# The masked keys' term of a causal attention, made from turned values, a reversed scan and a spread weight

## What is computed

```python
att = jnp.einsum('bhqd,bhkd->bhqk', q, k) / np.sqrt(HEAD_DIM)
causal = jnp.tril(jnp.ones((T, T), dtype=bool))
att = jnp.where(causal, att, 0.0)
att = jax.nn.softmax(att, axis=-1)
out = jnp.einsum('bhqk,bhkd->bhqd', att, v)
```

## Time and profile before

| | us |
|---|---|
| median of 3 runs (1337.8 to 1341.09) | 1340.07 |
| span of the profiled execution, first to last instruction | 1332.9 |
| median less that span | 7.2 |
| token stage, up to the attention's first matmul | 268.6 |
| PE busy | 1165.0 (87%) |
| DVE busy | 949.8 (71%) |
| ACT busy | 747.9 (56%) |
| POOL busy | 364.2 (27%) |
| mean granted TensorE clock | 0.950 |

### The profile page before, as it was taken

One profiled execution on the slowest core, in us unless ns is written; L12 is line 12 of the kernel. 1 busy time (PEld: TensorE's weight loads), 2 busy tenths in 40 slices (PEclk: granted clock), 3 DMA queues, 4 the chain that ended last, 5 costly groups with the idle time before them and its releaser, 6 DMA issues.

```text
span 1332.9 us, 26802 instructions
## 1 busy us (share of the span) xinstructions
PE 1165.0 (87%) x7680; PEld 508.3 (38%) x7680; DVE 949.8 (71%) x1921; ACT 747.9 (56%) x1553; POOL 364.2 (27%) x716
## 2 busy tenths in 40 slices
PE   2999488889998799879896999699879996999998
PEld 1666355433343243324332333233323332333345
DVE  5777388878688668866785689568766885689822
ACT  1544233256765576557564766476547664766673
POOL 6121011333323132413132223222232233224221
PEclk9999699989999899989997999799889998999999
DMA  2446933371007100810063006300540054002023
GB/s 87 142 158 169 178 111 111 111 92 45 6 1 98 43 6 3 97 43 6 4 82 59 6 2 79 62 6 3 65 77 6 2 64 77 6 2 73 5 84 115
DMA packets 59124, 79.55 MB, mean 60 GB/s; under 512 B 6112, under 2 KB 48480, under 8 KB 57952
## 3 DMA queue, kind: packets, MB, share of 16 engines
q1 hardware_dynamic: 57824, 73.56, 27.8%
q0 software_dynamic: 1152, 4.19, 1.0%
HBM read 43.78 MB, written 29.36 MB: 55 GB/s over the span
## 4 chain that ended last, share of the span: by engine, by line
PE 56%; DMA 10%; DVE 7%; issue 3%; ACT 2%; SPq 1%; DVEq 1%; ACTq 0%; POOL 0%; POOLq 0%
PE ps_s L1046 16%; PE ps_o L1060 16%; PE ps_m L209 14%; DMA q_op<-shift_t 10%; DVE part_max L220 5%; PE ps_o L1070 2%; PE ps_m L1092 2%; PE ps_m L213 2%; ACT probs L928 2%; PE ps_x L1037 1%; PE ps_x L1038 1%; DVE row_max L233 1%; DVE turned L963 1%; SPq L775 1%; PE ps_x L1023 1%
## 5 line engine op out<-in xcount | busy, mean ns | idle before, releaser
L220 DVE TENSOR_REDUCE part_max<-ps_m 128x1 f32<-128x512 f32 (+3 forms) x1200 | 669.1, 603 | 249.0 <-PE ps_m L213 130.7
L928 ACT ACTIVATE probs<-ps_s 128x512 f32<-128x512 f32 (+3 forms) x1280 | 614.0, 535 | 365.2 <-PE ps_s L1046 359.9
L1046 PE MATMUL ps_s<-q_op,k_op 99*128 99x512 bf16 (+3 forms) x1280 | 444.1, 360 | 75.7 <-DMA q_op<-shift_t 62.7
L209 PE MATMUL ps_m<-k_op,q_op 96*128 96x512 bf16 (+3 forms) x1200 | 411.2, 359 | 23.5 <-DVE part_max L220 20.4
L1060 PE MATMUL ps_o<-probs,v_sb 128*32 128x512 f32 (+3 forms) x2560 | 304.1, 548 | 0.0
L876 POOL TENSOR_SCALAR_AFFINE_SELECT probs<-probs 128x128 f32<-128x128 f32 x512 | 146.3, 295 | 567.6 <-ACT probs L928 560.0
L1046 PEld LDWEIGHTS ps_s<-q_op,k_op 99*128 99x128 bf16 x1280 | 123.4, 99 | 388.2 <-ACT probs L928 225.3
L209 PEld LDWEIGHTS ps_m<-k_op,q_op 96*128 96x128 bf16 x1200 | 118.8, 99 | 145.3 <-DVE part_max L220 90.8
L843 POOL TENSOR_TENSOR diag_weight<-ident,masked_weight 128x2048 f32<-128x2048 f32 x32 | 115.5, 3610 | 122.1 <-ACT masked_weight L895 122.1
L213 PE MATMUL ps_m<-mask,ident 128*128 128x128 bf16 x470 | 103.4, 222 | 0.1
L1060 PEld LDWEIGHTS ps_o<-probs,v_sb 128*32 128x32 f32 x2560 | 51.0, 109 | 89.5 <-issue 47.0
(11 more groups left out here) (85 smaller groups left out, 831.6 us busy)
## 6 DMA issues: line engine op xcount, KB each, us to landing
parts_d<-parts SPq DMA_DIRECT2D x48, 256.0 KB, 3.0
q_op<-parts_d SPq DMA_DIRECT2D x48, 256.0 KB, 14.2
k_op<-parts_d SPq DMA_DIRECT2D x48, 256.0 KB, 15.8
vpad_d<-v_pad SPq DMA_DIRECT2D x32, 256.0 KB, 3.2
v_sb<-vpad_d SPq DMA_DIRECT2D x8, 1024.0 KB, 25.8
x_in<-x SPq DMA_DIRECT2D x8, 512.0 KB, 4.6
ffn_d<-ffn SPq DMA_DIRECT2D x8, 512.0 KB, 3.2
attn_t<-normed SPq DMA_DIRECT2D x128, 32.0 KB, 2.0
```

Source lines behind the costliest of these rows:

```text
L209: last = pe.matmul(ps_m[:, f % ring, 0:width], self.q_op[0:ROWS, p, h, q0:q0 + P], self.k_op[0:ROWS, p, h, pc * CH:pc * CH + width], start ...
L220: dve.tensor_reduce(self.part_max[:, u % 2, h * SUB + s, pc:pc + 1], ps_m[:, f % ring, 0:width], AX_X, ALU.max).then_inc(self.piece_reduce ...
L928: act.activation(probs[:, slot % PRING, 0:width], ps_s[:, slot % SRING, 0:width], ACT.Exp).then_inc(probs_ready, 1)
L1046: pe.matmul(ps_s[:, slot % SRING, 0:CH - q0], k_op[0:KROWS, p, h, kt * P:(kt + 1) * P], q_op[0:KROWS, p, h, u * CH + q0:(u + 1) * CH], sta ...
```

## The change

The values are kept a second time with channels on the partitions. For each chunk PE makes two more turned projections (`project_v_turned`), ACT copies them, SP stores them to `vt_d`. For each group four transfers of 128 KB (`load_turned`) bring the four heads' rows to `vt_sb`, each to 16 partitions; the other 16 rows of each head hold ones, for the count. DVE runs a scan from the last key to the first (`scan_after`, four instructions of 512 columns a group, in unit 2 of the group before, for the first group in chunk 7), so `after_t` holds the sum of the values after each query. PE spreads the turned shift over each head's 32 rows by one bf16 matmul a unit (`spread_shift`, 12 rows to 128, 512 columns), ACT takes its exponential (`keep_weight`), POOL multiplies it with `after_t` (`weigh_masked`) and adds it to the kept sums (`add_masked`), both 128 x 512 float32. `masked_keys`, `sum_suffix`, `add_up_after` and `spread_weight` go, with what ACT did for them. The scratch `prev_term` goes too (DVE writes into `mixed`), with no instruction more or less.

```diff
+SPREAD_AT = {(3, 6): 0, (3, 12): 1, (1, 3): 2, (2, 9): 3}
+SCAN_AT = {(2, 4): 3, (2, 6): 2, (2, 8): 1, (2, 10): 0}
+FIRST_SCAN_AT = {1: 3, 3: 2, 5: 1, 7: 0}
...
+    def load_turned(self, sp, i, p):
+        for h in range(GH):
+            sp.dma_start(self.vt_sb[h * HW:h * HW + HD], self.vt_in[i, p, h]).then_inc(self.vt_loaded, 16)
+
+    def scan_after(self, dve, p, n, c):
...
+        dve.tensor_tensor_scan(out, self.one[:].broadcast_to([P, count]), self.vt_sb[:, c * CH + 1:end + 1][:, ::-1], carry,
+                               ALU.mult, ALU.add).then_inc(self.scanned, 1)
...
+            def project_v_turned(n, k):
+                pe.wait_ge(rest_ready, n * 4 + 3 + k)
+                for cc in range(CC):
+                    last = pe.matmul(ps_qk[:, k], w_in_sb[:, cc, 2 * C + k * P:2 * C + (k + 1) * P],
+                                     xn_t[:, cc, 1:CH + 1], start=(cc == 0), stop=(cc == CC - 1))
+                last.then_inc(vt_projected, 1)
...
                     for j in range(2, 4):
                         project_qk(n, j)
                         pieces(c, 2 + j)
+                    for k in range(CC):
+                        project_v_turned(n, k)
...
                     pe.wait_ge(k_act_ready, n + 1)
                     for half in range(2):
-                        pe.wait_ge(parts_ready, n * 4 + 3 + half)
+                        pe.wait_ge(vt_kept, n * 2 + half + 1)
...
                 if not last:
-                    sp.wait_ge(out_ready, unit_of(i, p, 0) + 1)
+                    sp.wait_ge(probs_used, used_before(i * 2 + p, 0))
                     ops.load_group(sp, i + p, 1 - p)
+                    sp.wait_ge(scanned, (i * 2 + p + 1) * NCH)
+                    ops.load_turned(sp, i + p, 1 - p)
                 place_shift(p, 2, unit_of(i, p, 2))
...
         def _(pool):
-            def spread_weight(u, n):
+            def weigh_masked(p, u, n, G):
                 pool.wait_ge(weight_ready, n + 1)
-                pool.tensor_tensor(diag_weight[:, u % 2], ident[:].unsqueeze(1).broadcast_to([P, GH * SUB, P]),
-                                   masked_weight[:, u].unsqueeze(2).broadcast_to([P, GH * SUB, P]),
-                                   ALU.mult).then_inc(diag_ready, 1)
+                pool.wait_ge(scanned, (G + 1) * NCH)
+                pool.tensor_tensor(masked[:, u], masked[:, u], after_t[:, p, u * CH:(u + 1) * CH],
+                                   ALU.mult).then_inc(masked_ready, 1)
+
+            def add_masked(u, n):
+                pool.wait_ge(masked_ready, n + 1)
+                pool.wait_ge(sums_kept, n + 2)
+                pool.tensor_tensor(sums[:, u % 2], sums[:, u % 2], masked[:, u], ALU.add).then_inc(sums_ready, 1)
...
             def group(i, p, first=False, last=False):
                 G = i * 2 + p
                 for u in range(NCH):
+                    weigh_masked(p, u, unit_of(i, p, u), G)
+                    if not (first and u == 0):
+                        add_masked((u - 1) % NCH, unit_of(i, p, u - 1))
...
                     for kt in range(SUB * u, SUB * u + SUB):
...
         def _(act):
+            def keep_weight(u, n):
+                act.wait_ge(spread_ready, n + 1)
...
+                act.activation(masked[:, u, 0:width], ps_x[:, 0:width], ACT.Exp).then_inc(weight_ready, 1)
...
         def _(pe):
-            def masked_keys(p, u, G):
-                pe.wait_ge(diag_ready, G * NCH + u + 1)
...
+            def spread_shift(u, n):
+                pe.wait_ge(shift_t_ready, n + 1)
+                pe.matmul(ps_x[:], ops.pick_head[:], shift_t[:, u % 2], start=True, stop=True).then_inc(spread_ready, 1)
```

More of the change, by code:

```diff
@@ L139, in __init__ @@
         self.v_sb = sb("v_sb", [P, 2, NT, GH * HW])
[L140 to L143, removed]
+        self.vt_sb = sb("vt_sb", [P, T])
+        self.after_t = sb("after_t", [P, 2, T])
+        self.one = sb("one", [P, 1])
+        self.pick_head = sb("pick_head", [3 * GH, GH * HW], BF16)
         self.mask16 = sb("mask16", [P, P], BF16)
@@ L179, in set_constants @@
                            base=-(P - 1), pattern=[[0, GH]], channel_multiplier=1).then_inc(self.consts_made, 1)
[L181 to L184, removed]
+        pool.wait_ge(ident_ready, 2)
+        pool.wait_ge(self.consts_made, 2)
+        rows = 3 * GH
+        by_part = [self.ident16[0:rows, k * GH:(k + 1) * GH].unsqueeze(2).broadcast_to([rows, GH, HW]) for k in range(3)]
+        pick = self.pick_head[:].rearrange("p (h w) -> p h w", w=HW)
+        pool.tensor_tensor(pick, by_part[0], by_part[1], ALU.add).then_inc(self.consts_made, 1)
+        pool.wait_ge(self.consts_made, 3)
+        pool.tensor_tensor(pick, pick, by_part[2], ALU.add).then_inc(self.consts_made, 1)
     def load_group(self, sp, i, p):
@@ L192, in load_group @@
         sp.dma_start(self.v_sb[:, p], self.v_in[i, p]).then_inc(self.v_loaded[p], 16)
[L194 to L201, removed]
+    def load_turned(self, sp, i, p):
+        for h in range(GH):
+            sp.dma_start(self.vt_sb[h * HW:h * HW + HD], self.vt_in[i, p, h]).then_inc(self.vt_loaded, 16)
+    def scan_after(self, dve, p, n, c):
+        dve.wait_ge(self.vt_loaded, (n + 1) * GH * 16)
+        end = (c + 1) * CH
+        if c < NCH - 1:
+            dve.wait_ge(self.scanned, n * NCH + NCH - 1 - c)
+            carry, count = self.after_t[:, p, end:end + 1], CH
+        else:
+            carry, end, count = 0.0, T - 1, CH - 1
+        out = self.after_t[:, p, c * CH:end][:, ::-1]
+        dve.tensor_tensor_scan(out, self.one[:].broadcast_to([P, count]), self.vt_sb[:, c * CH + 1:end + 1][:, ::-1], carry,
+                               ALU.mult, ALU.add).then_inc(self.scanned, 1)
     def score_piece(self, pe, ps_m, ring, f, p, base):
@@ L753, in stage_attention @@
         USED = PRING // GH
-        q_op, k_op, v_sb, after, v_after = ops.q_op, ops.k_op, ops.v_sb, ops.after, ops.v_after
-        keys_after, ones, row_max, shift = ops.keys_after, ops.ones, ops.row_max, ops.shift
-        q_loaded, k_loaded, after_ready, max_ready, shift_ready = (
-            ops.q_loaded, ops.k_loaded, ops.after_ready, ops.max_ready, ops.shift_ready)
-        total = [buf[:, 0, half * 8:half * 8 + 8].rearrange("p (s a) f -> p s (a f)", s=SUB)
-                 for buf in (v_sb, v_after) for half in range(ORING // 2)]
+        q_op, k_op, v_sb, after_t, shift = ops.q_op, ops.k_op, ops.v_sb, ops.after_t, ops.shift
+        q_loaded, k_loaded, scanned, shift_ready = ops.q_loaded, ops.k_loaded, ops.scanned, ops.shift_ready
+        total = [v_sb[:, 0, half * 8:half * 8 + 8].rearrange("p (s a) f -> p s (a f)", s=SUB) for half in range(2)]
+        total += [ops.vt_sb[:, half * SUB * C:(half + 1) * SUB * C].rearrange("p (s c) -> p s c", s=SUB) for half in range(2)]
         block = ctx.enter_context(nc.Block())
@@ L866, in group @@
                             load_chunk(n)
-                    if u == NCH - 1 and not last:
-                        spread_weight(0, unit_of(i, p, NCH))
                     for kt in range(SUB * u, SUB * u + SUB):
```

173 lines of the change are left out of this document (77 added, 96 removed).

## The result

The change makes the kernel slower: 1375.77 us (median of 4 runs, 1373.07 to 1377.3) against 1339.26 for the kernel before in the same comparison, a ratio of 1.0268 with a 95% interval of 1.0248 to 1.0287. The prediction was 1365, range 1346 to 1388. The profiled span grew from 1332.9 to 1371.3 us, by 38.4, and the mean granted TensorE clock fell from 0.950 to 0.935. The medians grew by 36.5: the median lies 6.4 us above the profiled span before (7.2 in the three runs that the prediction had) and 4.5 after. So the prediction is 13.1 us short on the span and 10.8 on the median.

A forecast was written before the change was run, and what follows sets the result against it. In groups 1 to 6 the shift store's landing behind SP's loads, then PE in units 2 and 3, was taken as the bound. Token stage +20.1 and attention +5.2 made +25.3 us on the span: 1365, range 1346 to 1388.

The forecast's parts named there:

- A: SP's issues and queue, groups 1 to 6: four added loads ahead of the shift store, +4.3 us a group, +25.8 in all.
- C: Units 2 and 3, from the shift store's landing: PE relieved of masked-key work, -4.3 us a group, -25.8 in all.
- The scans: DVE in unit 2 and chunk 7: 0.75 us each, costing +0.5 us a group and +2.0 in chunk 7.
- rival 4: DVE's scan takes two passes' time, 1.4 us each: +11 us, total 1376; chance 0.16.
- D: From unit 3's end to `normed`: POOL's selects wait behind its product and add, +1.9 us a group, +11.4 in all.
- The token stage: Added turned projections: +10.9 us in chunks 0 to 3, chunk 4 hidden, +7.2 in 5 to 7, scans +2.0; sum +20.1.
- Group 0 and the tail: Attention's start and end: group 0 about +0.4 us; from group 6's unit 2 to the end -6.6.
- The 1.5 us for `row_max`: Group 7: DVE's 0.2 us `row_max` no longer meets POOL's 3.6 us product, -1.5 us.
- 1: Rival: the vt loads run at the values' rate, costing +1.5 us a group; total 1348; chance 0.14.
- 2: Rival: PE's relief counts in full and the queue does not hold the shift back; total 1296; chance 0.03.
- 3: Rival: the net is nothing, vt loads free and POOL's wait half as long; total 1334; chance 0.04.
- 5: Rival: POOL's delay of `normed` and the token stage at their upper bounds, +13 us; total 1378; chance 0.15.

The follow-up runs named there:

- e1_vt_behind: Kernel after the change, with SP issuing the four loads of turned values behind unit 2's shift store instead of ahead of it: 1351.63 us, ratio 1.0104.
- e8_half_reduces: Kernel after the change, with DVE taking each maximum over only the upper half of its piece: 1330.57 us, ratio 0.9931.
- e6_before_relief: Kernel before the change, with PE's suffix sums and `masked_keys` narrowed and nothing added: 1303.08 us, ratio 0.9719.
- e7_short_scans: Kernel after the change, with scans of 32 columns instead of 512 from the third group on: 1371.34 us, ratio 1.0229.
- e3_selects_first: Kernel after the change, with POOL taking unit 0's first four selects ahead of its two products: 1365.83 us, ratio 1.0204.
- e2_narrow_proj: Kernel after the change, with the matmuls projecting the turned values 16 columns wide instead of 512: 1370.62 us, ratio 1.0232.

## Why the prediction came out as it did

*A, total right, in part by luck.* +24.4 us for +25.8. The step took 4.3 a group, the q and k loads' rate, against a bound of 1.5; with the loads behind the store 3.2 a group went (`e1_vt_behind`), between the two. The other 5.2 us come from the same loads taking longer to land, which no term had and no run explains; without them the forecast of A would have been 6.6 us too high.

*C, mechanism right, size wrong.* The step was -4.3 us a group; measured, -1.6. By its own terms unit 3 was to give 4.0 (suffix sums 3.5, one `masked_keys` 1.0, less two spreads) and unit 2 0.3. Unit 3 gave 2.2 us in every group, 10.7 of the 16.3 us that C fell short. The sentence that failed is "DVE has 9 of 52.5 us to spare in unit 3, so I count all of it": in the shorter unit DVE is busy 42.6 of 49.9, and its pieces are the next bound (`e8_half_reduces`: 46.9 with PE's work as it was; `e6_before_relief`: 49.2 with the relief and nothing added). The other 5.6 lie in unit 2, of which 3.4 in group 0, whose unit 2 took 31.5 us before and now starts behind a wait of 4.4 us and takes 34.6. The long waits of the other groups are no part of the miss: their unit 2 took 2.2 to 3.0 us more than group 0's before the change as well. The last 2.2 us, in groups 1 to 5, have no cause shown.

*The scans, price wrong, consequence small.* 1.28 us each, not 0.75: 1284 ns against 683 ns for the two-input pass. It is the price of rival 4, whose total of 1376 is the measured one for another reason: that rival spent 8.4 us more on them in the attention, and `e7_short_scans` leaves room for about 0.4 a group in all. The Trainium skill (DVE: opcode table, instruction layouts, handler registers and perf-mode slots, section "Datapath and trigger behaviour") says that the scan's program runs at half throughput. The trace agrees: 1284 / 683 = 1.9.

*D, right.* +8.8 for +11.4, 1.5 a group instead of 1.9, through the queue the step named: the first `weigh_values` of a group waits 1.9 us for POOL's selects behind the add, and moving the selects ahead gives 8.4 us of it back (`e3_selects_first`).

*The token stage, size right, its parts not.* +17.3 for +20.1. To the first projection of chunk 4 (119.8 us before) it is +12.3 (predicted 10.9); chunks 4 to 6 cost 0.3 together, not 4.8, and the wait for `k_op` went from 18.6 to 14.7; chunk 7 costs 4.7 (predicted 4.4). In chunks 0 to 3 the step reckoned with PE's time alone, and `e2_narrow_proj` shows that this was not the whole reason: with two thirds of that time gone, 10.5 of the 12.3 us stay. And `e8_half_reduces` shows DVE's maxima in what follows: with them halved the first projection of chunk 4 comes 0.6 us earlier and the stage ends 11.0 earlier. So the sum came out by parts that made up for each other.

*Group 0 and the tail.* Group 0's store, whose unit 2 "had a few us to spare", is now late by those 4.4 us; they are in the +0.7. From the last landing to the end -3.3 came of -6.6. It is C's size again: in group 6 units 2 and 3 gave 1.5 and not 4.3, in group 7 they gave 0.3. The 1.5 us for `row_max` were too little: unit 1 of group 7 went from 25.4 to 22.0, and one `masked_keys` less is 1.0 of that.

*The rivals.* 1 is out by A, 2 by the waits, 3 by both. 5 (D and the token stage at their upper bounds) is out by the table; the measured time near its 1378 comes from C.

## What to carry to other kernels

PE's relief is worth what the next engine in that stretch leaves of it: ask what waits for that engine in the shorter stretch, not how idle it was in the old one. DVE was busy 42.6 of 49.9 us and still held unit 3. Before transfers are added to a queue, the small store that something waits for goes ahead of the large loads; here that move was worth 63 us before the change and 130 after it, and turned the change from +36 into -31 us. And an engine's queue decides when a short instruction runs: selects behind a product that nothing needs yet, or a 0.16 us maximum in the shadow of a 3.6 us product, cost several times their length.

## What the hardware showed that was not expected

- A small DVE instruction with two inputs in SBUF stood until GpSimd's product was done, 1.67 us for 0.16 us, mean 555 ns over the span before and 169 ns after the change. The Trainium skill (SBUF — State Buffer, section "Who interferes with whom") says that such a DVE instruction contends with a GpSimd instruction that reads SBUF; the trace agrees.
- The granted clock fell behind short stands too: PE busy 1.5 of 3 us was followed by 5 us at 0.66, and 1.03 of 3 us in the token stage by 5.3 us at 0.68. Behind the long wait it was 0.50 for 4.5 us and 0.89 for 5 more. The price of a wait did not grow with its length: the same unit 2 of groups 0 to 6 took 31.7 to 31.8 us behind no wait or 1.1 us, 34.6 behind 4.4, 34.3 to 34.8 behind 13.2 to 14.7, and 33.4 to 34.6 behind 16.2 to 17.8.
- Narrowing a float32 matmul from 512 to 16 columns took its busy time from 0.48 to 0.16 us a record (30.5 and 10.4 us in 64 records), a third and not a thirtieth.
